# A recurrent scan with attention beside it: half of a projection one step earlier, the widening ahead of the second product, a residual behind the cell's scan

## The reference

```python
x = x + deformable_conv(group_norm(x))            # 3x3, 64 -> 64
t = tokens(x)                                     # 4 x 256 x 64
t = t + attention_block(layer_norm(t))            # below
t = t + lstm(layer_norm(t))                       # 256 steps, 4 rows, 64 units

# attention_block, 8 heads of 32
y  = softmax(q @ k.T * 32 ** -0.5) @ v @ w_out.T + b_out
x1 = layernorm(y + x) * g1 + b1
ff = (gelu(y @ w1.T) * (y @ wv.T)) @ w2.T
return layernorm(ff + x1) * g2 + b2

# lstm, one step
i, o = sigmoid(x_i + h @ V_i), sigmoid(x_o + h @ V_o)
g = tanh(x_g + h @ V_c)
c_new = h * c + i * g                             # h multiplies c; there is no use of f
h_new = o * tanh(c_new)
```

## Time and profile before

| | us |
|---|---|
| median of three runs | 381.32 |
| lowest, highest of the three | 380.89, 381.32 |
| the profiled execution | 380.76 |
| its span | 378.9 |
| PE busy, share of the span | 350.2, 92% |
| DVE busy | 239.1, 63% |
| ACT busy | 225.1, 59% |
| POOL busy | 56.8, 15% |

### The profile page before, as it was taken

How to read it: one execution, slowest core, us unless ns; L and a number is a source line. 1 busy time by engine, 2 the same in 40 slices (tenths; PEclk the granted TensorE clock), 3 DMA queues, 4 the chain that set the end, 5 groups by cost and what they waited for, 6 DMA issues and landing times.

```text
span 378.9 us, 15328 instructions
## 1 busy us (share of the span) xinstructions
PE 350.2 (92%) x5881; PEld 192.3 (51%) x5934; DVE 239.1 (63%) x1230; ACT 225.1 (59%) x1072; POOL 56.8 (15%) x124
## 2 busy tenths in 40 slices
PE   7999999899999999999999989999999999988886
PEld 3566675544554555455545544554455445543332
DVE  3678755556666666675766576756766666664443
ACT  2767664527754865586458646864685477543442
POOL 5001112212201221121112111211121112010000
PEclk9999999999999999999999999999999999999999
DMA  7000000000000000000000000000000000000000
GB/s 233 2 1 13 9 16 19 9 1 4 2 3 4 6 3 3 2 8 2 3 6 3 5 2 6 3 3 3 7 3 4 3 5 5 2 2 6 2 3 6
DMA packets 4807, 3.98 MB, mean 10 GB/s; under 512 B 3837, under 2 KB 4286, under 8 KB 4734
## 3 DMA queue, kind: packets, MB, share of 16 engines
q1 hardware_dynamic: 4432, 2.45, 2.4%
q10 hardware_dynamic: 302, 0.55, 0.4%
HBM read 2.20 MB, written 0.26 MB: 7 GB/s over the span
## 4 chain that ended last, share of the span: by engine, by line
PE 65%; DVE 15%; ACT 12%; issue 7%; DMA 1%; POOL 0%; DVEq 0%; POOLq 0%
PE bank L790 18%; PE bank L399 9%; PE bank L570 8%; DVE bank L1344 6%; PE bank L586 5%; DVE H L1354 5%; PE bank L485 5%; ACT bank L979 4%; ACT bank L972 4%; PE bank L473 4%; PE bank L607 4%; ACT E L895 2%; PE bank L687 2%; PE bank L721 1%; PE bank L699 1%
## 5 line engine op out<-in xcount | busy, mean ns | idle before, releaser
L399 PE MATMUL bank<-FB 128*128 128x512 bf16 (+3 forms) x433 | 125.7, 361 | 9.0 <-issue 7.8
L790 PEld LDWEIGHTS bank<-H,VW 64*32 64x32 f32 x3060 | 52.1, 106 | 105.0 <-DVE H L1354 103.1
L972 ACT ACTIVATE bank<-bank 64x8 f32<-64x8 f32 x256 | 37.6, 147 | 87.7 <-PE bank L790 84.8
L790 PE MATMUL bank<-H,VW 64*32 64x4 f32 x3060 | 74.3, 176 | 12.1 <-DVE H L1354 1.7
L1344 DVE TENSOR_TENSOR_SCAN bank<-bank,SU 64x12 f32<-64x12 f32 x256 | 48.5, 190 | 49.9 <-ACT bank L972 46.8
L1354 DVE SCALAR_TENSOR_TENSOR H<-TO,bank 64x4 f32<-64x4 f32 x256 | 40.8, 159 | 44.8 <-ACT bank L979 34.1
L376 POOL TENSOR_SCALAR E<-E,rinv 128x256 f32<-128x256 f32 x62 | 29.8, 482 | 125.8 <-DVE rinv L1142 125.8
L399 PEld LDWEIGHTS bank<-FB 128*128 128x128 bf16 x486 | 37.9, 98 | 20.9 <-issue 2.8
L979 ACT ACTIVATE bank<-bank 64x4 f32<-64x4 f32 x256 | 38.4, 150 | 16.1 <-DVE bank L1344 0.3
L976 ACT ACTIVATE TO<-bank 64x4 f32<-64x4 f32 x256 | 43.8, 171 | 6.1
L1338 DVE SCALAR_TENSOR_TENSOR SU<-H,bank 64x4 f32<-64x4 f32 x256 | 41.3, 161 | 9.1
(11 more groups left out here) (122 smaller groups left out, 307.4 us busy)
## 6 DMA issues: line engine op xcount, KB each, us to landing
AW<-in_attn_w SPq DMA_DIRECT2D x1, 768.5 KB, 7.1
DW<-in_dcn_w SPq DMA_DIRECT2D x1, 288.0 KB, 5.3
X<-in_x_fm SPq DMA_DIRECT2D x1, 256.0 KB, 3.1
X<-in_x_fm ACTq DMA_DIRECT2D x1, 256.0 KB, 5.0
T<-T0T SPq DMA_DIRECT2D x16, 16.0 KB, 1.8
Y<-YT SPq DMA_DIRECT2D x16, 16.0 KB, 1.8
out_dram<-OUT SPq DMA_DIRECT2D x8, 32.0 KB, 1.4
K<-in_consts ACTq DMA_DIRECT2D x1, 181.0 KB, 3.3
```

Source lines behind the costliest of these rows:

```text
L399: nc.tensor.matmul(idle[:, 0:n], FB[:, 0:P], FB[:, 0:n], start=True, stop=True)
L790: mm = nc.tensor.matmul(gate_out(m, gate, r, slice(B * s, B * (s + 1))), VW[0:C, gate, r], H[0:C, (STEPS * m + s - 1) % RING, :], start=Fa ...
L972: nc.scalar.activation(GT[:, :, 1:3].rearrange("p b g -> p g b"), b_cell[m % 2][0:C, 0:2 * P].rearrange("p (g s b) -> p g s b", g=2, b=B)[ ...
```

## The change

For the tiles 1 to 7 (the first tile's attention lies before the scan and keeps its order):
- The copy of head group 1 is cut in two. DVE copies three images at o = 17 (`HEADS_PART`, semaphore `o_part`) and the fourth at o = 19. The last weighing, which writes the same bank, now waits for `o_part`.
- The first product of the turned projection is issued at o = 17, behind the fill, where it was at o = 18. Step 18 keeps the weighing and one product of `project`.
- At o = 20 the first widening is issued ahead of the second product of `project`.
- `planned` gets the new costs, so the fill is 1152 columns at o = 17 (before 1536), 256 at 18 (before none), 256 at 19 (before 768), and none at 20 as before.
- R2 is made behind the scan of step 25 (`SUMMED_2`, in `beside_tanh`) and no longer ahead of the scan of step 26.

```diff
+HEADS_PART = 17
+SUMMED_2 = 25
...
-NS_PROJECT, NS_WIDEN, NS_NARROW, NS_INPUT, NS_PRELOAD, NS_STATES = 430, 545, 420, 140, 600, 210
+NS_HEADS, NS_AHEAD, NS_BESIDE, NS_PROJECT, NS_WIDEN, NS_NARROW, NS_INPUT, NS_PRELOAD, NS_STATES = 200, 260, 350, 430, 545, 420, 140, 600, 210
...
+                if u == NU - 1 and m >= 1:
+                    pe.wait_ge(o_part, m)
...
-                    ns += NS_TURN * (o in TURN_AT) + NS_PROJECT * (o in (PROJECT, PROJECT + 1)) + NS_PROJECT // 2 * (o == PROJECT + 2)
+                    ns += NS_TURN * (o in TURN_AT) + NS_AHEAD * (o == PROJECT - 1) + NS_BESIDE * (o == PROJECT) + (NS_PROJECT + NS_HEADS) * (o == PROJECT + 1) + NS_PROJECT // 2 * (o == PROJECT + 2)
...
+                    if o == PROJECT - (m > 0):
+                        project_turned(m, 0)
                     if o == PROJECT:
-                        project_turned(m, 0)
                         (project_turned if m == 0 else project)(m, 1 if m == 0 else 0)
                     if o == PROJECT + 1:
                         (project if m == 0 else project_turned)(m, 0 if m == 0 else 1)
-                    if o == PROJECT + 2:
+                    if m == 0 and o == PROJECT + 2:
                         project(m, 1)
                     if o == WIDEN:
                         widen(m, 0)
+                    if m > 0 and o == PROJECT + 2:
+                        project(m, 1)
...
-            def heads_out(m, hg):
+            def heads_out(m, hg, images):
 
-                dve.wait_ge(pv_mm, NU * m + B * (hg + 1))
+                dve.wait_ge(pv_mm, NU * m + B * hg + images.stop)
                 dve.wait_ge(y_mm, m)
-                nc.vector.tensor_copy(O[:, hg, :, :].rearrange("p t b -> p b t"),
-                                      b_pv[:, P * hg:P * (hg + 1)].rearrange("p (b t) -> p b t", b=B)).then_inc(o_done, 1)
+                return nc.vector.tensor_copy(O[:, hg, :, images].rearrange("p t b -> p b t"),
+                                             b_pv[:, P * hg:P * (hg + 1)].rearrange("p (b t) -> p b t", b=B)[:, images])
...
-                    if m > 0 and o in HEADS:
-                        heads_out(m, HEADS.index(o))
+                    if m > 0 and o == HEADS[0]:
+                        heads_out(m, 0, slice(0, B)).then_inc(o_done, 1)
+                    if m > 0 and o == HEADS_PART:
+                        heads_out(m, 1, slice(0, B - 1)).then_inc(o_part, 1)
+                    if m > 0 and o == HEADS[1]:
+                        heads_out(m, 1, slice(B - 1, B)).then_inc(o_done, 1)
...
-                    if o == NARROWED:
-                        dve.wait_ge(ff_mm, m + 1)
-                        dve.wait_ge(x1_done, m + 1)
-                        nc.vector.scalar_tensor_tensor(out=R2[:], in0=b_t[:, 0:C], scalar=0.5, in1=X1[:],
-                                                       op0=ALU.mult, op1=ALU.add).then_inc(r_done, 1)
...
             def beside_tanh(g):
 
                 for m, o in at(g):
+                    if o == SUMMED_2:
+                        dve.wait_ge(ff_mm, m + 1)
+                        dve.wait_ge(x1_done, m + 1)
+                        nc.vector.scalar_tensor_tensor(out=R2[:], in0=b_t[:, 0:C], scalar=0.5, in1=X1[:],
+                                                       op0=ALU.mult, op1=ALU.add).then_inc(r_done, 1)
```

More of the change, by code:

```diff
@@ L237, in hybrid_kernel @@
             "q_mm", "q_done", "s_mm", "s_max", "e_done", "e_inv", "e_norm", "et_mm", "et_sb", "pv_mm", "o_done"))
-        yf_mm, o_early = sem("yf_mm"), sem("o_early")
+        yf_mm, o_early, o_part = sem("yf_mm"), sem("o_early"), sem("o_part")
         y_mm, r_done, ay_done, h_mm, ge_done, ff_done, ff_mm, t_mv, t_rs, t1_done, ln3_done, xt_mm, xt_done = (
```

## The result

Twenty runs of each kernel on one chip: the changed kernel has a median of 385.39 us (380.88 to 396.00), the kernel before 381.35 (380.89 to 396.14). The comparison leaves the slowest runs out, one of the kernel before (396.14) and five of the changed one, of which only two (395.73 and 396.00) look like that one, and gives a ratio of 1.0059, interval 1.0033 to 1.0084; the medians of all runs give 1.0106. By either figure the change makes the kernel slower. I had forecast 379.8 with a range up to 380.7.

What follows compares the result with a forecast made beforehand. One recurrent chain (H, gates on PE, tanh on ACT, scan on DVE, tanh, H) bounds the kernel; four stalls removed less 0.04 for step 18 give -0.204 per block, -1.43 over seven, so 379.8 us, range 379.0 to 380.7.

Steps and rivals of the forecast that it cites:

- Steps 19, 20, 21 and 26: Long steps of seven blocks, late by 0.074, 0.033, 0.095 and 0.042 us; all four were to become undisturbed.
- step 18: New stall from PE's added work in step 17: about 0.04 us longer, bounds nothing to 0.10.
- the partial copy: DVE's copy of three of four images in step 17: takes 0.33 us, hidden ahead of the scan by 0.02.
- AY and Gelu: ACT operations delaying the gates' tanh: AY to start about 0.97 into step 19, Gelu 1.03 into step 20.
- no matmul for 0.095: Gap on PE at a change of shape, expected ahead of the turned projection in step 17: 0.095 us.
- The transpose without a gap: LN's transpose on PE, labelled 128*64 like the projection, starts without idle time; row against the assumed gap.
- rival D: Less fill in steps 17 to 20 lowers the clock to 1.2 GHz: slower, +1.3, 382.6 us; chance 0.04.
- the sum: Per block -0.074 - 0.033 - 0.095 - 0.042 + 0.04 = -0.204 us; seven blocks -1.43.
- 0.39 for one fill step: Estimated gate delay at half clock in a step with 1536 fill columns; one per block costs 2.7 us.
- the last block's steps run at full clock: Ground against a clock fall: the last block's steps have only gates and fill and stay at 1.00.
- five late single steps: Five single steps outside the four stalls, longer by 0.04 to 0.13 us, said to follow no pattern.
- the four stalls: Lateness of steps 19, 20, 21 and 26: 0.244 us per block, 1.71 over seven blocks, the whole prize.

Runs made afterwards that it cites:

- Experiment 7: Changed kernel plus 512 fill columns behind step 19's turned product, 22 DVE memsets at the start, fill 1024 in step 17 and 384 in 18; 379.22 us, ratio 0.9955.
- experiment 2: Kernel before with only step 19's fill cut to 256 columns from 768, no instruction moved; median 387.05 us, ratio 1.0037.
- experiment 8: Changed kernel plus 256 fill columns behind the second half of the turned projection in step 19; 380.41 us, ratio 0.9988.
- experiment 1: Changed kernel plus 512 fill columns behind the second half of the turned projection in step 19; 380.70 us, ratio 0.9986.
- experiment 6: Changed kernel plus 512 fill columns behind step 19's turned product and 21 one-column DVE memsets at the start; 381.15 us, ratio 1.0002.

## Why the prediction was wrong

The forecast of the chain was right step for step. Steps 19, 20, 21 and 26 are 1.14, step 18 is longer by 0.04 with the gates at 0.09 after H's end, the partial copy takes the 0.33 I gave it and stays off the scan, AY and Gelu start where I put them. Experiment 7 undid the 0.04 by ending PE's work of step 17 sooner. By the Trainium skill, "TensorEngine Tiling (Array Packing)", Key Properties, a change of tiling mode drains TensorE; the trace agrees at the projection, with no matmul for 0.095. The transpose without a gap stays unexplained.

The step that failed is rival D. I had put the cost of a lower clock at nothing in the sum, and it was 4.5 us in the trace. I had its place, and its price too low: 0.39 for one fill step in each block, where the trace has up to 0.57 for each of two steps in four blocks, the first of them by the widening and only the second by the fill. I gave it a chance of 0.04, on two grounds. One was that the last block's steps run at full clock. But nearly all of those hold 1536 fill columns, which is much more than step 19 was left with, so they bear out nothing about a step with 256. The row that would have spoken was not there: among the steps of the kernel before whose matmul rows are complete, none is as light as step 19 became (0.93 of 1.14 busy; there 1.04 or more). That called for a bound and not for a dismissal. The other was my reading of the Trainium skill, "TensorE: Matmul & The Clock Gate", What's actually happening, that the clock falls only behind idle time. The trace disagrees with it: PE is busy for 0.93 of 1.14 in step 19, works through step 20, and the clock still falls in step 21. The words "no step is without gates and fill" were wrong besides: step 20 has no fill in either kernel. What the runs put in place of this step of the prediction: the lighter fill of step 19 alone, with the order as before, brings the fall (experiment 2, 387.05), and 256 columns put back in that step prevent it (experiment 8, 380.41). The standstill that rival D named as the reason is not borne out by its length, and the exact condition stays open.

Cutting fill in step 17 made room for the product that was moved there; no run kept the fill of that step. In step 19 the 512 columns had been removed for nothing: the product needed to start before 0.77, and the same columns fit behind it (experiment 1, step 20 stays 1.14).

The sum was also short of one term. I wrote that five late single steps follow no pattern. They follow the number of the DVE instruction. The change adds two DVE records per block, a copy and its wait, and so deals the places anew: 1.24 us where before had 0.39. Even without a fall the changed kernel would by this sum have gained about 0.6 and not 1.43; experiments 1 and 8, which have no fall, gained 0.48 and 0.51. Of the gain of experiment 7, 1.71 are the stalls and 0.1 the places. Two smaller slips stand in the prediction: the sum gives 379.89 and I said 379.8 without a reason, and a fall would have used up the gain from 0.20 us per block on, not from 0.24.

## What to carry to other kernels

- A dummy matmul that seems to be only cover can be what keeps the clock up. Whoever shortens one should look for the step that is left with the least work on PE, put the columns into that step behind the work instead of ahead of it, and judge by many runs: here three runs of twenty were free of a fall.
- In a kernel whose chain crosses an engine every microsecond, adding or taking away instructions moves the places at which that engine is late. One such shift was worth 1.8 us here, more than the 1.71 of the four stalls. Before a small change is judged, compare the late single steps, and try a few no-ops in both.

## What the runs showed of the hardware

- The granted clock fell to 1.2 GHz although PE was idle for at most 0.27 us at a time by its rows in the steps ahead of the fall (0.17 in experiment 2). Gaps of 0.33 and 0.34 behind steps with 1536 fill columns passed at full clock (experiment 6). The fall came one to two steps behind the thin step, and 256 columns in that step prevented it in eleven runs of eleven.
- Every late single step has a DVE record with number 63 modulo 128 at it. When the record was H, the step was 0.21 to 0.23 us late, when it was the scan 0.08 to 0.10. Another operation on the place cost 0.22 to 0.25 (steps 111, 15 and 220 in the traces of the changed kernel and of experiment 6) or nothing (steps 108 and 164 of experiment 6), the product of H with the old cell 0.04 or nothing, a wait 0.12 to 0.14 (steps 37 and 131) or, mostly, nothing. An 8 KB packet of the instruction queue follows each such record of the scan within 1 us, also where the places were shifted. That the engine is late because it passes into a newly fetched block is the likely reading and not measured by itself.
- The undisturbed step differs from trace to trace: 1.1375 us in some, 1.1394 to 1.1396 in others, on one chip both, and 1.1384 in the three traces from another. From the lowest to the highest that is 0.54 us over the scan. What sets it stays open.
